# Four transformer layers written as one program block: weights in two places, the next attention's first steps placed inside the MLP

## The reference, cut to what matters

```python
h = patches @ conv_w + pos_embed                    # 64 images, 197 tokens, width 128
for i in range(4):
    y = layernorm(h, ln1_w[i], ln1_b[i])
    q, k, v = split_heads(y @ qkv_w[i] + qkv_b[i])  # 8 heads of 16
    o = softmax(q @ k.T * 16 ** -0.5) @ v
    h = h + (o @ proj_w[i] + proj_b[i])
    y = layernorm(h, ln2_w[i], ln2_b[i])
    h = h + (gelu(y @ fc1_w[i] + fc1_b[i]) @ fc2_w[i] + fc2_b[i])
h = layernorm(h, norm_w, norm_b)
...                                                 # the two later stages, unchanged
```

## Time and profile before

| | |
|---|---|
| median of 3 runs | 4391.66 us (4374.48 to 4392.35) |
| the profiled execution's own time | 4389.62 us |
| its span | 4387.8 us |
| busy | TensorE 82%, VectorE 59%, GpSimd 51%, ScalarE 43% of the span |
| mean granted TensorE clock | 0.923 of 2.4 GHz |

### The profile page before, as it was taken

The page is one execution under the profiler, slowest core; times in us unless marked ns, Lnnn a source line. Parts: engine busy times, 40 slices in busy tenths (PEclk is TensorE's granted clock), DMA queues, the critical chain, the costliest instruction groups (busy, mean ns, idle before and its releaser), DMA issues. The chain is left out here.

```text
span 4387.8 us, 94079 instructions
## 1 busy us (share of the span) xinstructions
PE 3618.4 (82%) x30906; PEld 2777.3 (63%) x30906; DVE 2582.0 (59%) x6605; ACT 1870.3 (43%) x3340; POOL 2255.2 (51%) x2633
## 2 busy tenths in 40 slices
PE   9779998849999776999884999977788787876973
PEld 9657776637777554777663777766333565654763
DVE  1357775536776445777553677745777587865210
ACT  0046665315666423666531566643233343321321
POOL 0066662535665335666253566624555464344776
PEclk9879999958999996999996899999999998998997
DMA  6466662026666005666301666600000122231332
GB/s 224 143 119 125 128 124 46 0 58 119 123 125 124 1 7 100 120 123 129 69 0 31 122 125 125 128 18 11 26 21 23 37 64 54 36 81 46 66 57 33
DMA packets 456034, 341.71 MB, mean 78 GB/s; under 512 B 70659, under 2 KB 440171, under 8 KB 455595
## 3 DMA queue, kind: packets, MB, share of 16 engines
q1 hardware_dynamic: 413635, 314.62, 34.8%
q0 software_dynamic: 27136, 16.42, 2.8%
q10 hardware_dynamic: 15008, 7.51, 0.7%
HBM read 227.69 MB, written 109.29 MB: 77 GB/s over the span
## 5 line engine op out<-in xcount | busy, mean ns | idle before, releaser
L584 DVE TENSOR_REDUCE a_neg_max<-a_S 99x4 f32<-99x788 f32 x1024 | 1003.5, 980 | 610.6 <-PE a_S L327 596.8
L467 ACT ACTIVATE a_probs<-a_St 99x792 f32<-99x792 f32 (+1 forms) x1024 | 850.3, 830 | 690.1 <-PE a_St L342 678.5
L342 PE MATMUL a_St<-a_q_st,a_k_st 99*99 99x198 bf16 (+1 forms) x4096 | 532.3, 252 | 87.8 <-DMA a_q_st<-a_max_rows 73.4
L327 PE MATMUL a_S<-a_k_st,a_q_st 96*99 96x197 bf16 x4096 | 560.1, 261 | 41.8 <-DVE a_neg_max L584 41.7
L327 PEld LDWEIGHTS a_S<-a_k_st,a_q_st 96*99 96x99 bf16 x4096 | 405.5, 130 | 270.3 <-DVE a_neg_max L584 224.4
L342 PEld LDWEIGHTS a_St<-a_q_st,a_k_st 99*99 99x99 bf16 (+1 forms) x4096 | 393.4, 127 | 119.9 <-DMA a_q_st<-a_max_rows 69.9
L357 PE MATMUL a_O<-a_probs,a_v_aug 99*32 99x198 f32 (+1 forms) x8192 | 467.0, 341 | 1.1 <-ACT a_probs L467 1.0
L357 PEld LDWEIGHTS a_O<-a_probs,a_v_aug 99*32 99x32 f32 (+1 forms) x8192 | 247.3, 110 | 86.7 <-issue 2.3
L679 PE MATMUL m_H<-m_yT,layer_w 128*128 128x396 f32 x512 | 211.3, 537 | 79.6 <-ACT m_yT L710 79.6
L721 POOL TENSOR_TENSOR h<-h,layer_rows 99x512 f32 (+1 forms) x128 | 162.6, 1270 | 217.3 <-DVE m_xn L746 217.3
L546 POOL CAST a_max_parts<-a_neg_max 99x32 bf16<-99x32 f32 x128 | 26.8, 210 | 461.3 <-DVE a_neg_max L584 461.3
(11 more groups left out here) (266 smaller groups left out, 7606.9 us busy)
## 6 DMA issues: line engine op xcount, KB each, us to landing
xpatch<-in_x SPq DMA_DIRECT2D x64, 594.0 KB, 3.7
spill_q<-a_parts SPq DMA_DIRECT2D x384, 99.0 KB
spill_k<-a_parts SPq DMA_DIRECT2D x384, 99.0 KB
a_k_st<-spill_k SPq DMA_DIRECT2D x128, 297.0 KB, 4.3
a_q_st<-spill_q SPq DMA_DIRECT2D x128, 297.0 KB, 6.4
a_k_st<-spill_k SPq DMA_DIRECT2D x128, 198.0 KB, 4.9
a_q_st<-spill_q SPq DMA_DIRECT2D x128, 198.0 KB, 6.7
a_k_st<-spill_k SPq DMA_DIRECT2D x128, 99.0 KB, 5.1
```

The costliest lines, as they stand in the source:

```text
L327: mm = nc.tensor.matmul(S[0:TC, j // 2, j % 2 * TB:j % 2 * TB + NTOK], q_st[p % 4][0:SPLIT, head, b * TB + c * TC:b * TB + (c + 1) * TC], ...
L342: mm = nc.tensor.matmul(St[0:keys, j // 2, j % 2 * TB:(j % 2 + 1) * TB], k_st[p][:, head, at:at + keys], q_st[p][:, head, b * TB:(b + 1) * ...
L467: nc.scalar.activation(probs[0:keys, u % 4, :].rearrange("p (x t) -> p x t", x=2), St[0:keys, :, 0:2 * TB], ACT.Exp).then_inc(s["probs"], 1)
L584: nc.vector.tensor_reduce(out.rearrange("p (x y) -> p x y", x=2), S[0:TC, :, 0:2 * TB].rearrange("p x (y t) -> p x y t", y=2)[:, :, :, 0:N ...
```

## The change

The three phases and the loop over layers become one function, `layers_phase`, with one block and one set of semaphores for all four layers; the counts run on from layer to layer (`at(l, x)` adds 32 for each layer). The layers are unrolled in the text, and in each the attention loop over steps 4 to 23 stays a hardware loop; the MLP has none any more.

- **Weights** have two places, chosen by the layer's parity. On SyncE layer l+1's three loads stand behind the last step of layer l's attention, with a wait for the MLP of layer l-1. The folding is cut into four pieces (`prep`), which stand behind MLP pairs 1, 2, 3 and 4 of the layer before; it uses PSUM bank `M1`.
- **The lead-in**: steps -6 to -1 of the next attention stand behind MLP pairs 9, 13, 17, 21, 25 and 29 (`PROLOGUE`), on every engine at the same place of its stream.
- **The MLP's first three steps** (-3, -2, -1) stand between the attention's last steps (30, 31, 32, 33).
- **PSUM**: attention and MLP now live at the same time, so the MLP takes attention's banks: its transpose `M2` (one bank for two), its first product `St` (two for four), its second `O` (one for two).
- The eight buffers of L574 and L575 and the identity are set once and not once a layer. The semaphore of the spill writes is split in two by parity. A layer's first transposed scores, its first product with v and its first k get a wait for the MLP before or for `prep`.

The arithmetic of every instruction stays as it was.

```diff
-def load_layer(nc, g, A, layer):
...
-def attention_phase(nc, g):
...
+LEAD = 6
+PROLOGUE = (9, 13, 17, 21, 25, 29)
+
+def layers_phase(nc, g, A):
...
+        w_all = [sb(f"w{p}", [128, 8 * D]) for p in range(2)]
+        cols_all = [sb(f"cols{p}", [128, 9]) for p in range(2)]
+        rows_all = [sb(f"rows{p}", [TC, 2 * D]) for p in range(2)]
...
+            def run(eng):
+                for k in range(4):
+                    prep(0, k)
+                for i in range(-LEAD, 0):
+                    step(0, i)
+                for l in range(DEPTH):
...
+                    step(l, PAIRS - 2)
+                    mlp(l, -3, -LEAD - 1)
+                    step(l, PAIRS - 1)
+                    mlp(l, -2, -LEAD - 1)
+                    step(l, PAIRS)
+                    mlp(l, -1, -LEAD - 1)
+                    step(l, PAIRS + 1)
+                    done = -LEAD - 1
+                    for k in range(PAIRS):
+                        mlp(l, k, done)
+                        if l + 1 < DEPTH:
+                            if 1 <= k <= 4:
+                                prep(l + 1, k - 1)
+                            if k in PROLOGUE:
+                                done += 1
+                                step(l + 1, done, at(l, k + 3))
...
+                        wait(pe, s["m_yT"], n + 1)
+                        for h in range(2):
+                            wait(pe, s["m_gelu"], 2 * (n - 1) + h + 1)
+                            nc.tensor.matmul(St[:, h, 0:PW], m.w1[:, h * 128:(h + 1) * 128], m_yT[n % 2][:],
+                                             start=True, stop=True).then_inc(s["m_fc1"], 1)
...
+                        wait(pe, s["m_gelu"], 2 * (n + 1))
+                        wait(pe, s["m_h"], n)
...
+                        wait(pe, s["m_xn"], n + 1)
+                        wait(pe, s["m_yT"], n)
+                        wait(pe, s["yT"], at(l + 1, done + 6))
+                        wait(pe, s["max_copied"], at(l + 1, done + 2))
...
-def mlp_phase(nc, g):
...
-        with nc.Fori(0, DEPTH) as layer:
-            load_layer(nc, g, A, layer)
-            attention_phase(nc, g)
-            mlp_phase(nc, g)
+    layers_phase(nc, g, A)
```

More of the change, by code:

```diff
@@ L321, in scores @@
+                def scores(l, i, p, even, u):
                     b, half, c = u // 4, u // 2 % 2, u % 2
@@ L522, in body, with mlp @@
                     if now:
-                        exp(i, 7)
-                steps(body)(act)
+                        exp(l, i, 7)
+                def mlp(l, k, done):
+                    m = layer_w[l]
+                    if 0 <= k + 1 < PAIRS:
+                        n = at(l, k + 1)
+                        for h in range(2):
+                            wait(act, s["m_fc1"], 2 * n + h + 1)
+                            wait(act, s["m_fc2"], n - 1)
+                            nc.scalar.activation(gl[n % 2][:, h, :], St[:, h, 0:PW], ACT.Gelu,
+                                                 bias=m.b1[:, h:h + 1]).then_inc(s["m_gelu"], 1)
+                    if 0 <= k + 2 < PAIRS:
+                        n = at(l, k + 2)
+                        wait(act, s["m_turned"], n + 1)
+                        wait(act, s["m_fc1"], 2 * (n - 1))
+                        nc.scalar.activation(m_yT[n % 2][:], M2[:, 0:PW], ACT.Copy).then_inc(s["m_yT"], 1)
```

613 lines of the change are left out of this document (307 added, 306 removed).

## The result

| | before | changed |
|---|---|---|
| median | 4392.01 us (4 runs, 4374.48 to 4394.90) | 4190.79 us (4 runs, 4178.56 to 4193.22) |
| the profiled execution's own time | 4389.62 us | 4193.22 us |
| mean granted clock | 0.923 | 0.943 |

The ratio is 0.9544, 95% interval 0.9513 to 0.9575. The forecast was 4183 us. Against the profiled execution's own time the changed kernel takes 196.4 us less, where the sum said 207.

The account below looks back on a forecast made before the run. No engine is busy throughout; the prediction looked for where all stand still, at the seams between phases. Savings of 147 (layer seams), 55 (MLP starts) and 5 us (before layer 0), 207 off 4389.6, gave 4183 us, range 4110 to 4250.

Parts of the forecast that it names:

- The seam: From one layer's last MLP sum to the next layer's first transposed scores: 47 us instead of 95.8, three times, saving 147 us.
- The steps: Lead-in steps -6 to -1 inside the MLP delay TensorE by nothing, 4, 5, 7, 11 and 12 us: together 39 us a seam.
- The clock: Idle gaps at lead-in steps lower TensorE's clock in the MLP: 4 us a seam, bounds nothing to some 20 us.
- The preparation: Folding of the next layer's weights behind four MLP pairs: TensorE's 5.22 us at half clock become 2.6, costing 3 us a seam.
- The way across: Between the last MLP sum and the next layer's first transposed scores only one score group remains: 1 us a seam.
- The queue that is late next: GpSimd after step -4's split: transpose two pairs later possible at 1558.3 us, wanted at 1558.1, called just hidden.
- The MLP start: Starting the MLP inside attention's end brings its first sum from 761.5 to 747.7 us: 13.8 us, four times, 55 us.
- Before layer 0: Memsets run beside the first weight load and its 4.5 us are covered: 5 us saved.
- PSUM: The MLP loses its second banks, but existing order already meets the new waits: no cost, 1.5 us to spare.
- Emptied pipeline: Rival: each of five steps also loses the MLP's fill, 54 us more a seam, time about 4346 us; chance 0.06.
- Low clock in the MLP: Rival: half clock costs 2.56 us a pair, up to 4511 us; chance 0.02 (some 70 pairs), 0.01 (about 81), 0.03 (more).
- Hidden steps: Rival: the lead-in steps hide almost wholly as other engines run ahead in the MLP, about 4117 us; chance 0.04.

Follow-up runs that it names:

- warm: Changed kernel plus throwaway bf16 matmuls in the lead-in steps of layers 1 to 3, into an idle PSUM bank: 4170.27 us, ratio 0.9490 to the kernel before.
- tail_undo: Changed kernel with only the overlap at each MLP's start undone, its first three steps again behind attention step 33: ratio 0.9627 to the kernel before.
- fine: Changed kernel with the six lead-in steps cut into pieces, one or two behind each of MLP pairs 1 to 31: 4052.36 us, ratio 0.9267 to the kernel before.

## Why the prediction was right, and where its terms were off

**The seam, three times 147 us.** Measured 141.1 (288.2 - 147.1). Its parts:
- *The steps, 39 us.* Near full clock (`warm`) a seam costs 39.2 us, the preparation's 0.3 us and the way of 0.7 us among it, so some 38 us for the steps: the term held within 1 us, and its five parts within 1.3 us (8.0, 10.6, 10.6, 14.2 and 16.05 us a pair, for 8.3, 9.3, 11.3, 15.3 and 16.3). With 8.92 us and 0.7 us in the two pairs behind for step -4, as it was at 1.00, the steps come to 37 us.
- *The clock, 4 us.* This is the term that was mis-sized: it cost 8 to 12 us in the profiled execution, of the 20 that the upper bound allowed. I took a value near the lower end because the MLP kept its clock with 14.5% idle; but a step is not a stretch of evenly spread idle time, it has one stand of 2.5 us and then rounds in which TensorE works a third of the time. The rows to go by were those of the old lead-in, at 0.50 throughout with TensorE busy 58%.
- *The preparation, 3 us.* It cost 0.28 us. I had counted TensorE's own work as exposed, though a piece of it fits the 0.67 us gap of each pair.
- *The way across, 1 us.* 0.15 us to the first transposed scores.

That the seam's 47 us came so near (49.6 us measured) is in part luck: the clock cost 4 to 8 us more than its term, the preparation and the steps some 4 us less than theirs.

**The queue that is late next.** I called GpSimd's root "just hidden" behind step -4, although my own numbers had the transpose possible at 1558.3 us and wanted at 1558.1, 0.2 us too late. Layer 1's MLP shows it just not hidden, in the one step -4 of this trace that ran at full clock:

```profile
1496.47 1.02 POOL L674 TENSOR_TENSOR a_m_rstd<-a_m_ve,neg_half 99x4 f32<-99x4 f32 x1
1497.52 0.69 DVE L801 TENSOR_TENSOR a_m_xn<-h,a_m_rstd 99x512 f32<-99x512 f32 x1 [2.52 <-POOL a_m_rstd L674]
...
1498.27 0.56 PE L522 MATMUL a_M<-ident,a_m_xn 99*128 99x99 f32 x4 [0.50 <-DVE a_m_xn L801]
```

VectorE waits for GpSimd's root, TensorE 0.50 us for VectorE, and the pair takes 4.88 us. The pipeline loses 0.6 us there and 0.1 us in the next pair, and is full again behind that. In the slower steps GpSimd has the time to catch up.

**The MLP start, four times 13.8 = 55 us.** Measured 51.1. The new length was right (11.0 forecast; 10.5, 10.5, 10.5, 12.0), but I multiplied the old length of layer 0, 24.8 us, by four, and the others had 22.4 to 23.7. `tail_undo` gives 10.3 of the 12.8 us a stage to the order alone. The start in the timeline of ScalarE:

```profile
744.12 1.28 ACT L599 ACT_TABLE_LOAD   x1
745.42 1.07 ACT L599 ACTIVATE a_gelu<-a_St,a_cols 128x396 f32<-128x396 f32 x2
```

The gelus start 0.02 us behind the 1.28 us of the table load, which itself starts 0.01 us behind the row ahead of it (a copy from 743.77 us on, 0.34 us long). The 1.38 us of drain that the Trainium skill (ScalarE: Activation LUTs, "What ACT_TABLE_LOAD costs") adds are not in these rows either, as in the earlier trace rows, and the forecast without them came out.

**Before layer 0, 5 us**: 4.9. **PSUM, nothing**: the fourth MLP, with half the banks, took 131.1 us (131.0 before) at a clock of 1.00. The Trainium skill (TensorE: Matmul & The Clock Gate, "A second HAM failure mode: psum-queue depth-cycling") lets the clock swing where matmul groups cycle through PSUM banks with short idles; in this window the trace disagrees. **Unrolling, nothing**: pairs of 4.28 us.

**The rivals.** Emptied pipeline: no, the pair behind a stretched one is 4.28 us, in one case 4.88. Low clock in the MLP: it came at the steps alone, and pairs away from them kept 4.28 us. Hidden steps: not in this change; but `fine` shows that the work can be hidden, where 38 us of step cost fell to 8. That is also below the 21 us that I had set as the steps' lowest price, TensorE's own work: I had counted this work as added to the pairs, and most of it fits their 0.67 us gaps, the same error as with the preparation. The reason I gave against it, that a step is in one piece, was right for this kernel and was a property of the change and not of the work.

Both errors promised too much (6 us in the seams, 4 us at the MLP starts), 10 us of 207 together. What no term spoke of, the attention stages (3.4 us shorter) and the stretch behind the fourth MLP (4.1 us longer), cancels out by chance: both differ by more than that from one execution to the next.

## What to carry to other kernels

Price a piece of work that is moved into another phase's in-order streams as a serial chain from its first wait to the next phase's first instruction, and bound the price by full clock and by the clock that the same work had when it stood alone; here about half of that difference was paid. Where it stands among the pairs matters little. Cut it into pieces about as long as the gap that the host phase has on its bounding engine: whole steps cost 46 to 50 us a seam, halves 45, pieces of one or two slots 9. That each producer and its consumer should fall into different pieces is what the traces suggest; it was not tried apart. Before moving one engine's share to remove a wait, add up that engine's idle time over all groups: if the order on the other engines is the same, the wait turns up elsewhere.
